# Second attention rewritten as one stream of 32 heads, its key tiles in pairs

## The chip, the cores and the metric

The kernel runs on one core of one Trainium2 chip. The metric is the time on the device in microseconds (us), the median of several runs. One execution was also recorded by the profiler.

## What is computed

The program is two layers of attention and expert feed-forward; the change touches the second attention alone:

```python
query, key, value = (aud_fea, img_fea, img_fea)   # _layernorm(x), ctx_1024, ctx_1024
q = _split_heads(query @ Wq.T, h)
k = _split_heads(key @ Wk.T, h)
v = _split_heads(value @ Wv.T, h)
attn = jnp.einsum('bhnd,bhmd->bhnm', q, k) * scale
attn = jax.nn.softmax(attn, axis=-1)
x = jnp.einsum('bhnm,bhmd->bhnd', attn, v)
```

There are 4 batches of 512 queries and 1,601 keys, 256 channels in 8 heads of 32. The result is added to x.

## The kernel before

`build` (L2156) puts four phases one behind the other, each a block with a barrier at its end: `attention0`, `experts`, `attention1`, `experts`. Here it is `attention1` (L1593) that matters.

**Precision.** Every float32 operand is split into two float16 parts, high and low. A product of projections takes three matmuls (high by high, high by low, low by high, `triple`, L1858). A head has only 32 channels, so the three products of a score are stacked along the contraction: `kst` holds per head 32 rows of high keys, 32 of low, 32 of high again, and a row of ones; `qst` holds high, high and low queries and a row with minus the maximum. One matmul with 97 rows (L1995) then gives the scores of 128 keys by 512 queries, less the maximum. The stacking is done by DMAs from SBUF to SBUF on the SP queue (L1727, L1735).

**Opening** (once). Weights are transposed and split, x of all 4 batches is normalised (L2040 to L2048), transposed, projected to queries and split (L1864 to L1889). Then the transposed and split context, the keys (L1893 on, events below NV0) and the values of batch 0 are made.

**A batch** (`batch`, L1931 on PE). First the values (13 tiles of keys), then the maxima of head 0 alone (L1962), then 8 heads. The maxima of head n+1 are spread over head n: 12 matmuls of 512 keys and 4 of 65 keys into `psA` (two buffers), reduced by DVE (L2108, L2103), combined to one column (`mc`, L2093), turned to a row by 4 transposes (L1946) and written by DVE into `qst` (L2097). Context and keys of the next batch are made during head 7 (`NEXT`); values and first maxima come after its end.

**A head** (`main`, L1987). For each of 13 tiles of keys (12 of 128, the last of 65): the score matmul into `psS` (4 buffers); ACT takes the exp twice, to float32 `pf` (L1831) and to float16 `ph` (L1833); POOL (10 tiles, L1774) or DVE (3 tiles, L2130) subtracts them to `pl`; PE multiplies `ph` and `pl` with the values into `psO` (L1971, L1973), five tiles behind the scores. Each tile of values holds high and low parts and a column of sums in 65 columns. After the last tile ACT copies `psO` to `of` (L1820); PE may overwrite `psO` only after this (`pe.wait_ge(s_oF, ...)` in `pv`). Four float32 matmuls with `fold` (L1983) add high and low and turn the result; DVE divides and adds to x (L2113, L2117). Heads 1 to 6 are a loop on every engine.

Of the kernel before, what the change touches and what calls it, by code (L numbers as in the profile page):

```python
# [24 lines left out]
P = 128  # L25
# [1567 lines left out]
def attention1(nc, X, identf, io):  # L1593

# [5 lines left out]
    NCK = len(KCH)  # L1606
    NQ = KC * NT // 4 + G * B
    NGC = KC * -(-JT // 4)
    NV0 = NGC + G * NCK
    NW = NV0 + JT  # L1610
    NA = 1 + ST * (NCK - 1)
# [3 lines left out]
    LAG = 5  # L1615
    PR = ring(JT, 7)
    SR = ring(JT, 4)
    R, NS = max(PR) + 1, max(SR) + 1
    VT = [2, 6, 10]
    GT = [j for j in range(JT) if j not in VT]  # L1620

    with ExitStack() as ctx:
        def sb(name, shape, dt=F32):
            return ctx.enter_context(nc.sbuf_tensor("c_" + name, shape, dt))

        def sem(name):
            return ctx.enter_context(nc.semaphore("c_" + name))

        wf = sb("wf", [P, 3, G, D])
        wth, wtl = sb("wth", [P, 3, KC, D], F16), sb("wtl", [P, 3, KC, D], F16)  # L1630
        st, mv = sb("st", [P, NT, 6]), sb("mv", [P, NT, 2])
        ve, mhalf, rstd = sb("ve", [P, NT]), sb("mhalf", [P, NT]), sb("rstd", [P, NT])
        qhs, qls = sb("qhs", [P, G, B * S], F16), sb("qls", [P, G, B * S], F16)
        qst = sb("qst", [P, H, B * S], F16)

        ltn = qst[:, 0:H // 2, :].rearrange("p h n -> p (h n)").bitcast(F32).rearrange("p (t c) -> p t c", c=D)
        lth = qst[:, H // 2:H // 2 + KC, :]
        ltl = qst[:, H // 2 + KC:H, :]
        kst = sb("kst", [P, H, M], F16)
        khs, kls = sb("khs", [P, G, M], F16), sb("kls", [P, G, M], F16)  # L1640
        vst = sb("vst", [P, JT, H, VC], F16)
        cx = sb("cx", [P, JT, D])
        cth, ctl = sb("cth", [P, KC, M], F16), sb("ctl", [P, KC, M], F16)
        mx, mc = sb("mx", [P, ST, NCK]), sb("mc", [P, ST])
        pf = sb("pf", [P, R, S])
        ph, pl = sb("ph", [P, R, S], F16), sb("pl", [P, R, S], F16)
        of = sb("of", [VC, S])
        fold = sb("fold", [VC, DH + 1])
        rl = sb("rl", [P, ST])

        psA = [ctx.enter_context(nc.psum_tensor(f"c_psA{i}", [P, 512], F32)) for i in range(2)]
        psS = [ctx.enter_context(nc.psum_tensor(f"c_psS{i}", [P, 512], F32)) for i in range(NS)]
        psO = ctx.enter_context(nc.psum_tensor("c_psO", [P, 512], F32))
        psM = ctx.enter_context(nc.psum_tensor("c_psM", [P, 512], F32))
        ring4 = psA + psS[0:2]
# [15 lines left out]
        s_wL = sem("wL")
        s_k = [sem(f"k{g}") for g in range(G)]
        s_aP = sem("aP")
        s_aF = sem("aF")
        s_mc = sem("mc")
        s_mT = sem("mT")
        s_mr = sem("mr")
# [7 lines left out]
        s_tP = sem("tP")  # L1685
        s_rl = sem("rl")
        s_tF = sem("tF")

        block = ctx.enter_context(nc.Block(no_gpsimd_drain=True))
        NCONST = 6  # L1690
        names = ("L1_xattn_Wq", "L1_xattn_Wk", "L1_xattn_Wv")

        def wait_low(eng, n, j):

            if j in VT:
                eng.wait_ge(s_pL, done(len(VT), n, VT.index(j)))
# [12 lines left out]
        NONE = [[] for _ in range(JT)]

        @block.sync
        def _(sp):
            for i, name in enumerate(names):
                sp.dma_start(wf[:, i, :, :], io[name].rearrange("(g p) c -> p g c", p=P)).then_inc(s_w, 16)
            def load_context(b):
                src = io["ctx_1024"][bass.ds(b, 1), :, :].rearrange("a m c -> (a m) c")
                sp.dma_start(cx[:, 0:MT - 1, :],
                             src[0:(MT - 1) * P, :].rearrange("(t p) c -> p t c", p=P)).then_inc(s_cx, 16)
                sp.dma_start(cx[0:MR, MT - 1, :], src[(MT - 1) * P:M, :]).then_inc(s_cx, 16)

            load_context(0)

            sp.wait_ge(s_uL, 3 + NQ)
            for h in range(H):
                r0 = (h % HG) * DH
                for piece, src in enumerate((qhs, qhs, qls)):
                    sp.dma_start(qst[piece * DH:(piece + 1) * DH, h, :], src[r0:r0 + DH, h // HG, :]).then_inc(s_q, 16)  # L1727
            def stack_keys(b):
                sp.wait_ge(s_sP, (b * H) * JT + JT)
                for g in range(G):  # L1730

                    sp.wait_ge(s_wL, done(NW, b, NGC + (g + 1) * NCK - 1))
                    for u in range(HG):
                        for piece, src in enumerate((khs, kls, khs)):
                            sp.dma_start(kst[piece * DH:(piece + 1) * DH, g * HG + u, :],  # L1735
                                         src[u * DH:(u + 1) * DH, g, :]).then_inc(s_k[g], 16)

            with sp.Fori(0, B - 1) as b:
                stack_keys(b)

                sp.wait_ge(s_wP, done(NW, b, NGC - 1))
                load_context(b + 1)
# [470 lines left out]
```

## Time and profile before

| | us |
|---|---|
| median of 3 runs | 2967.51 (2966.61 to 2968.86) |
| the profiled execution | 2967.55 |
| its span in the profile | 2965.7 |
| second attention, from the first load to the last write (L1714 to L2117) | 1836.4 to 2534.9 |

PE is TensorE's matmuls, PEld its weight loads, DVE VectorE, ACT ScalarE, POOL GpSimd, SP the queue that issues most DMAs. Starts are us from the span's start. In a timeline a line is: start, duration, engine, line of the kernel, instruction, tile written<-tiles read, count, and in brackets the idle time before it with what ended it. Matmuls overlap: one lasts 0.38 us, but the next may start 0.22 us after it, so costs on PE are read as the distance of starts.

### The profile page before, as it was taken

The page shows a single profiled execution, that of the slowest core. Times are in us where ns is not written, and L with a number is a line of the kernel's source. Part 1 is how long each engine was busy: PE and PEld are TensorE (multiplying, and loading weights), DVE is VectorE, ACT ScalarE, POOL GpSimd, SP SyncE. Part 2 cuts the span into 40 slices and gives each one's busy share as a digit, 9 for nine tenths or more (in the row PEclk, how much of TensorE's full clock was granted, in tenths as well). Part 3 has the DMA queues.
Part 4 walks back from the last instruction along what each step waited for, and adds up shares of the span by engine and source line. Part 5 has one row for each costly group of instructions (what it writes and reads, how often), then busy time and mean ns, then how long its engine had stood idle before and what let it go on. Part 6 is the DMA issues. An engine that isn't in the chain of part 4 may idle for free. (4 is left out here: it accounts for less than half of the span.)

```text
span 2965.7 us, 51867 instructions
## 1 busy us (share of the span) xinstructions
PE 2521.8 (85%) x15253; PEld 1505.1 (51%) x15380; DVE 1938.1 (65%) x3676; ACT 1728.1 (58%) x3155; POOL 1535.5 (52%) x1359
## 2 busy tenths in 40 slices
PE   4999999999999999999945991688888888379992
PEld 2455555555555555555424881344344444258882
DVE  5778677776777776677754644675767677656443
ACT  3556656566555665555523750387786868357661
POOL 2576766676676765665744005075665747320004
PEclk9999999999999999999966995799898999579996
DMA  4000000000000000000025413401002010543113
GB/s 130 1 1 1 23 1 1 1 1 23 1 1 1 1 1 1 1 1 1 1 89 180 146 39 97 99 1 30 26 3 52 0 34 0 203 160 117 45 46 93
DMA packets 83500, 122.54 MB, mean 41 GB/s; under 512 B 11139, under 2 KB 67285, under 8 KB 83349
## 3 DMA queue, kind: packets, MB, share of 16 engines
q1 hardware_dynamic: 72020, 86.23, 9.7%
q0 software_dynamic: 9472, 30.16, 3.0%
q10 hardware_dynamic: 1856, 4.19, 0.4%
q8 instruction: 89, 1.46, 0.2%
q14 instruction: 63, 0.51, 0.1%
HBM read 73.23 MB, written 34.34 MB: 36 GB/s over the span
## 5 line engine op out<-in xcount | busy, mean ns | idle before, releaser
L396 POOL TENSOR_TENSOR a_acc<-a_acc,a_pf 128x512 f32<-128x512 f32 (+1 forms) x480 | 644.8, 1343 | 388.0 <-ACT a_pf L524 367.8
L1774 POOL TENSOR_TENSOR c_pl<-c_pf,c_ph 128x512 f16<-128x512 f32 x320 | 386.8, 1227 | 284.7 <-ACT c_ph L1833 282.3
L524 ACT ACTIVATE a_pf<-a_psS 128x1024 f32<-128x1024 f32 (+1 forms) x288 | 281.2, 976 | 303.6 <-PE a_psS L663 300.1
L813 DVE TENSOR_TENSOR a_pl<-a_pf,a_ph 128x512 f16<-128x512 f32 x448 | 404.6, 912 | 27.5 <-ACT a_ph L530 27.5
L789 DVE TENSOR_REDUCE a_mx<-a_psA 128x1 f32<-128x512 f32 x512 | 344.5, 684 | 49.0 <-PE a_psA L600 42.7
L1270 POOL DMA_INDIRECT f_xn<-f_yrows,f_gidx x64 | 60.7, 949 | 506.5 <-DMA f_yrows<-f_xn 487.6
L1831 ACT ACTIVATE c_pf<-c_psS 128x512 f32<-128x512 f32 (+1 forms) x416 | 255.9, 615 | 114.0 <-PE c_psS L1995 110.6
L2108 DVE TENSOR_REDUCE c_mx<-c_psA 128x1 f32<-128x512 f32 x384 | 251.3, 684 | 53.0 <-PE c_psA L1962 51.2
L530 ACT ACTIVATE a_ph<-a_psS 128x1024 f16<-128x1024 f32 (+1 forms) x288 | 281.0, 976 | 0.0
L1833 ACT ACTIVATE c_ph<-c_psS 128x512 f16<-128x512 f32 (+1 forms) x416 | 257.4, 619 | 0.0
L784 DVE TENSOR_TENSOR a_vl<-a_psA,a_vh 128x256 f16<-128x256 f32 (+1 forms) x272 | 115.0, 423 | 167.4 <-ACT a_vh L469 164.4
L1130 DVE TENSOR_TENSOR f_xn<-f_xn 128x256 f16<-128x256 f32 x320 | 132.3, 422 | 130.9 <-ACT f_xn L1106 126.4
L685 PE MATMUL a_psO<-a_pl,a_vh 128*128 128x512 f16 (+1 forms) x544 | 206.7, 380 | 6.9 <-POOL a_pl L401 6.9
L679 PE MATMUL a_psO<-a_ph,a_vh 128*128 128x512 f16 (+1 forms) x544 | 206.9, 380 | 1.0 <-DVE a_ol L818 1.0
L542 PE MATMUL a_psS<-a_qh,a_kh 128*128 128x512 f16 (+1 forms) x544 | 206.6, 380 | 0.9 <-ACT a_mrow L485 0.8
L680 PE MATMUL a_psO<-a_ph,a_vl 128*128 128x512 f16 (+1 forms) x544 | 206.7, 380 | 0.0
L543 PE MATMUL a_psS<-a_ql,a_kh 128*128 128x512 f16 (+1 forms) x544 | 206.7, 380 | 0.0
L544 PE MATMUL a_psS<-a_qh,a_kl 128*128 128x512 f16 (+1 forms) x544 | 206.5, 380 | 0.0
L600 PE MATMUL a_psA<-a_kh,a_qh 128*128 128x512 f16 x512 | 194.3, 380 | 4.7 <-DVE a_kl L778 1.2
L778 DVE SCALAR_TENSOR_TENSOR a_kl<-a_psA,a_bkv,a_kh 128x512 f16<-128x512 f32 (+1 forms) x160 | 105.3, 658 | 133.7 <-ACT a_kh L463 133.6
L1035 PE MATMUL f_psH<-f_xh,f_w 128*128 128x256 f16 x648 | 178.4, 275 | 15.3 <-ACT f_xn L1106 11.7
L1971 PE MATMUL c_psO<-c_ph,c_vst 128*65 128x512 f16 (+1 forms) x416 | 160.8, 386 | 22.7 <-ACT c_of L1820 22.7
(340 smaller groups left out, 6395.2 us busy)
## 6 DMA issues: line engine op xcount, KB each, us to landing
f_stage<-in_L_ffn_w SPq DMA_DIRECT2D x16, 1024.0 KB
f_stage<-in_L_ffn_W SPq DMA_DIRECT2D x16, 1024.0 KB
f_xn<-f_xrows SPq DMA_DIRECT2D x41, 256.0 KB, 2.8
f_yrows<-f_xn SPq DMA_DIRECT2D x40, 256.0 KB, 2.2
c_kst<-c_khs SPq DMA_DIRECT2D x64, 100.1 KB, 2.2
f_xrows<-f_zero POOLq DMA_DIRECT2D x1, 6400.0 KB, 26.4
a_cx<-in_ctx SPq DMA_DIRECT2D x4, 1536.0 KB
c_cx<-in_ctx SPq DMA_DIRECT2D x4, 1536.0 KB
```

The lines of the kernel that those rows point to most:

```text
L396: g.tensor_tensor(acc[0:k, p, :], acc[0:k, p, :], pf[0:k, q % RF, i, :], ALU.add).then_inc(s_acc, 1)
L524: act.activation(pf[0:r, q % RF, 0:k, :], psS[q % 2][0:r, 0:k, :], ACT.Exp, scale=SCALE).then_inc(s_pF, 1)
L530: act.activation(ph[0:r, q % RP, 0:k, :], psS[q % 2][0:r, 0:k, :], ACT.Exp, scale=SCALE).then_inc(s_pH, 1)
L543: pe.matmul(out, hi, xl_, start=False, stop=False)
L679: pe.matmul(psO[:, :], vh[0:r, g % 2, j, vs], ph[0:r, q % RP, i, :], start=(j == 0), stop=False)
L680: pe.matmul(psO[:, :], vl[0:r, g % 2, j, vs], ph[0:r, q % RP, i, :], start=False, stop=False)
L789: v.tensor_reduce(mx[:, n % 2, it, c:c + 1], ps[:, 0:KCH[c][1]], AX.X, ALU.max).then_inc(s_fr, 1)
L813: v.tensor_tensor(pl[0:r, q % RP, i, :], pf[0:r, q % RF, i, :], ph[0:r, q % RP, i, :], ALU.subtract).then_inc(s_pL, 1)
L1774: g.tensor_tensor(pl[0:r, PR[j], :], pf[0:r, PR[j], :], ph[0:r, PR[j], :], ALU.subtract).then_inc(s_pG, 1)
L1831: act.activation(pf[0:r, PR[j], :], psS[SR[j]][0:r, :], ACT.Exp, scale=SCALE).then_inc(s_pF, 1)
L1833: act.activation(ph[0:r, PR[j], :], psS[SR[j]][0:r, :], ACT.Exp, scale=SCALE).then_inc(s_pH, 1)
L2108: v.tensor_reduce(mx[:, it, c:c + 1], psA[what % 2][:, 0:cn], AX.X, ALU.max).then_inc(s_aF, 1)
```

## The change

`attention1` is written anew, in the form that `attention0` has already: no loops, every engine walks the same list. A head is 7 units, six of two key tiles and one of the last 65 keys. On PE a unit has four places: after each of its two scores and after each of the two values that are multiplied there; items are put in these places.

- Scores of a pair go to one `psS` of two banks (two such buffers, three `psA` buffers for all other items, one `psO`); ACT takes exp over 128x1024 at once. Values are multiplied 4 units behind the scores.
- Of the 12 full tiles POOL subtracts 10 and DVE 2. The unit of 65 keys is neither split nor subtracted: ACT writes one exp `pw` in float32, and one float32 matmul multiplies it with float32 values `vf`.
- The copy of `psO` to `of` goes from ACT to DVE (`out_copy`), division is one DVE multiply of 128x128 into `yt`, and POOL adds `yt` to x (`add_to_x`).
- Context, keys, values and queries of batch b+1 (25 items `T`, `K`, `V`, `N`, `Q`, 24 of which pass ACT and all DVE) are spread over heads 0 to 5 of batch b. Maxima of the next batch's first head are made in head 7, like any other's. `kst`, `qst`, `vst` are double for this. x is normalised batch by batch. The context is loaded in pieces of 512 rows into two buffers.
- SP's order is: 4 context loads of batch b, then `stack(b)` with 48 DMAs, then the loads of batch b+1.
- POOL sets two rows of ones (`kst`), before it was one.

```diff
-    LAG = 5
-    PR = ring(JT, 7)
-    SR = ring(JT, 4)
-    R, NS = max(PR) + 1, max(SR) + 1
-    VT = [2, 6, 10]
-    GT = [j for j in range(JT) if j not in VT]
...
+    UNITS = [(j, j + 1) for j in range(0, JT - 1, 2)] + [(JT - 1,)]
+    U = len(UNITS)
+    NB = 3
+    LAG, LATE, RF, RP = 4, 1, 4, 7
+    ON_DVE = {(4, 1), (5, 1)}
+    TOP = U - 1
...
+    WHOLE = U - 1
+    STACK = 6 * 16
...
+    def keys_and_values(b):
+        out = []
+        for c in range(NK):
+            out += [("T", b, c, k) for k in range(KC) if k < parts(c)]
+            out += [("K", b, c, g) for g in range(G) if g < parts(c)]
+            out += [("V", b, u) for u in range(2 * c, min(2 * c + 2, U))]
+        return out
+    def queries(b):
+        return [("N", b, 0), ("N", b, 1), ("Q", b, 0), ("Q", b, 1)]
+    MAXIMA = [(it, c) for c in range(NK - 1) for it in range(ST)]
+    M_AT = [(0, 0), (0, 2), (0, 3), (1, 0), (1, 2), (2, 0), (2, 2), (2, 3), (3, 0), (3, 2), (4, 0), (4, 2)]
+    PREP_AT = [(h, u, p) for h in range(6) for u, p in ((1, 1), (4, 1), (5, 1), (6, 1))]
+    PREP_AT = [(h, u, p) for h, u, p in PREP_AT if (h, u) >= (0, LAG + 1)]
+    def head_items(n):
+        at = [[[] for _ in range(4)] for _ in range(U)]
+        if n + 1 < NH:
+            for (u, p), (it, c) in zip(M_AT, MAXIMA):
+                at[u][p].append(("M", n + 1, it, c))
+            at[TOP - 1][0].append(("L", n + 1))
+            at[TOP - 1][3].append(("X", n + 1))
+        if n >= 1:
+            at[LAG][2].append(("F", n - 1))
+        b, h = divmod(n, H)
+        if b + 1 < B:
+            todo = keys_and_values(b + 1) + queries(b + 1)
+            for i, what in enumerate(todo):
+                hh, u, p = PREP_AT[i * len(PREP_AT) // len(todo)]
+                if hh == h:
+                    at[u][p].append(what)
+        return at
+    OPEN = [("W", 0), ("W", 1), ("W", 2)] + keys_and_values(0)
+    OPEN[9:9] = queries(0)
+    FIRST = [("M", 0, it, c) for it, c in MAXIMA] + [("L", 0), ("X", 0)]
+    AT = [head_items(n) for n in range(NH)]
+    CLOSE = [("F", NH - 1)]
...
+            def stack(b):
+                if b >= 2:
+                    sp.wait_ge(s_sP, uid((b - 1) * H, 0))
+                sp.wait_ge(s_fr, after_dve(("Q", b, G - 1)))
+                for h in range(H):
+                    g, r0 = h // HG, (h % HG) * DH
+                    sp.wait_ge(s_fr, last_keys(b, g) + 1)
+                    for piece, (k, q) in enumerate(((khs, qhs), (kls, qhs), (khs, qls))):
+                        rs = slice(piece * DH, (piece + 1) * DH)
+                        sp.dma_start(kst[rs, b % 2, h, :], k[r0:r0 + DH, g, :]).then_inc(s_stack[h], 16)
+                        sp.dma_start(qst[rs, b % 2, h, :], q[r0:r0 + DH, g, :]).then_inc(s_stack[h], 16)
+            for b in range(B):
+                for c in range(NK):
+                    load_context(b, c)
+                stack(b)
...
+            def low(q, i):
+                r = rows1(tiles_of(q)[i])
+                g.wait_ge(s_pH, high(q))
+                g.tensor_tensor(pl[0:r, q % RP, i, :], pf[0:r, q % RF, i, :], ph[0:r, q % RP, i, :],
+                                ALU.subtract).then_inc(s_pG, 1)
+            def lows(q):
+                for i in range(len(tiles_of(q))):
+                    if (q % U, i) not in ON_DVE and q % U != WHOLE:
+                        low(q, i)
+            def add_to_x(n):
+                b, h = divmod(n, H)
+                g.wait_ge(s_fr, after_dve(("F", n)))
+                xs = X[:, b * ST:(b + 1) * ST, h * DH:(h + 1) * DH]
+                g.tensor_tensor(xs, xs, yt[:, n % 2, :, :], ALU.add).then_inc(s_x, 1)
...
+                    k, r = len(UNITS[u]), rows1(UNITS[u][-1])
+                    places = AT[n][u]
+                    for what in places[0]:
+                        item(what)
+                    act.wait_ge(s_sP, q + 1)
+                    if q >= RF:
+                        if low_dve(q - RF):
+                            act.wait_ge(s_pL, low_dve(q - RF))
+                        act.wait_ge(s_pG, low_pool(q - RF))
+                    if u == WHOLE:
+                        if n >= 1:
+                            act.wait_ge(s_pv, uid(n - 1, WHOLE) + 1)
+                        act.activation(pw[:, :], psS[q % 2][0:r, 0, :], ACT.Exp, scale=SCALE).then_inc(s_pF, 1)
+                    else:
+                        act.activation(pf[0:r, q % RF, 0:k, :], psS[q % 2][0:r, 0:k, :], ACT.Exp,
+                                       scale=SCALE).then_inc(s_pF, 1)
+                    for what in places[1]:
+                        item(what)
+                    if u != WHOLE:
+                        if q >= RP:
+                            act.wait_ge(s_pv, q - RP + 1)
+                        act.activation(ph[0:r, q % RP, 0:k, :], psS[q % 2][0:r, 0:k, :], ACT.Exp,
+                                       scale=SCALE).then_inc(s_pH, 1)
+                    for what in places[2] + places[3]:
+                        item(what)
...
+            def score(n, u, i):
+                q, j = uid(n, u), UNITS[u][i]
+                b, h = divmod(n, H)
+                r = rows1(j)
+                if i == 0:
+                    if q >= 2 and (q - 2) % U == WHOLE:
+                        pe.wait_ge(s_pF, q - 1)
+                    elif q >= 2:
+                        pe.wait_ge(s_pH, high(q - 2))
                     if u == 0:
...
+                        pe.wait_ge(s_fr, after_dve(("X", n)))
+                ins = pe.matmul(psS[q % 2][0:r, i, :], kst[0:KR, b % 2, h, j * P:j * P + r], qst[0:KR, b % 2, h, :],
+                                start=True, stop=True)
+                if i == len(UNITS[u]) - 1:
+                    ins.then_inc(s_sP, 1)
+            def value(q, i):
+                n, u = divmod(q, U)
+                b, h = divmod(n, H)
+                j = UNITS[u][i]
+                r = rows1(j)
+                if u == WHOLE:
+                    pe.wait_ge(s_pF, q + 1)
+                    if h == 0:
+                        pe.wait_ge(s_fr, after_dve(("V", b, u)))
+                    pe.matmul(psO[0:VC, :], vf[0:r, b % 2, h, :], pw[:, :], start=False,
+                              stop=True).then_inc(s_pv, 1)
+                    return
+                if i == 0:
+                    pe.wait_ge(s_pH, high(q))
+                    if u == 0 and n >= 1:
+                        pe.wait_ge(s_oF, n)
+                if h == 0 and i == 0:
+                    pe.wait_ge(s_fr, after_dve(("V", b, u)))
+                w = vst[0:r, b % 2, j, h, :]
+                pe.matmul(psO[0:VC, :], w, ph[0:r, q % RP, i, :], start=(j == 0), stop=False)
+                if i == 0:
+                    if low_dve(q):
+                        pe.wait_ge(s_pL, low_dve(q))
+                    pe.wait_ge(s_pG, low_pool(q))
+                ins = pe.matmul(psO[0:VC, :], w, pl[0:r, q % RP, i, :], start=False, stop=False)
+                if i == len(UNITS[u]) - 1:
+                    ins.then_inc(s_pv, 1)
...
+            def low(q, i):
+                if q < 0 or i >= len(tiles_of(q)) or (q % U, i) not in ON_DVE:
+                    return
+                r = rows1(tiles_of(q)[i])
+                v.wait_ge(s_pH, high(q))
+                v.tensor_tensor(pl[0:r, q % RP, i, :], pf[0:r, q % RF, i, :], ph[0:r, q % RP, i, :],
+                                ALU.subtract).then_inc(s_pL, 1)
+            def out_copy(n):
+                v.wait_ge(s_pv, uid(n, U - 1) + 1)
+                if n >= 1:
+                    v.wait_ge(s_it, IDX[("F", n - 1)] + 1)
+                v.tensor_copy(of[:, :], psO[0:VC, :]).then_inc(s_oF, 1)
```

## Rows read from the trace of the kernel before

**Rows 1.** The page, part 1: busy time of the engines
```profile
PE 2521.8 (85%) x15253; PEld 1505.1 (51%) x15380; DVE 1938.1 (65%) x3676; ACT 1728.1 (58%) x3155; POOL 1535.5 (52%) x1359
```
**Rows 2.** Windows: stretch, length; busy PE, PEld, DVE, ACT, POOL; granted clock; DMA share, GB/s
```profile
1836.40:1925.97 89.57, 51.64 (x264) 30.07 (x265) 58.35 (x111) 25.18 (x49) 15.49 (x9) 0.73 0.42 109
...
2086.93:2247.90 160.97, 137.50 (x690) 69.31 (x691) 111.98 (x213) 123.03 (x246) 96.74 (x80) 0.95 0.10 25
...
2408.90:2534.90 126.00, 107.59 (x509) 52.56 (x507) 89.27 (x167) 107.33 (x214) 96.53 (x80) 0.97 0.00 0
...
200.00:1400.00 1200.00, 1189.37 (x6679) 648.57 (x6785) 877.59 (x1453) 724.00 (x1090) 813.96 (x675) 1.00 0.01 4
```
**Rows 3.** Timeline of PE in steady heads: start, us, instruction, idle before
```profile
1948.81 0.38 PE L1973 MATMUL c_psO<-c_pl,c_vst 128*65 128x512 f16 x1
1949.02 0.98 PE L1983 MATMUL c_psM<-c_fold,c_of 65*128 65x33 f32 x8
1949.84 0.38 PE L1995 MATMUL c_psS<-c_qst,c_kst 97*128 x1
...
1954.66 0.60 PE L1946 MATMUL c_psM<-identf,c_mc 128*1 128x128 f32 x4 [1.18 <-DVE c_mc L2093]
...
1963.35 0.40 PE L1971 MATMUL c_psO<-c_ph,c_vst 128*65 128x512 f16 x1 [0.83 <-ACT c_of L1820]
```
**Rows 4.** Timelines of PE: keys and values of a batch, and a float32 group of the first attention
```profile
2055.03 0.39 PE L1859 MATMUL c_psA<-c_cth,c_wth 128*128 128x512 f16 x1 [1.50 <-DVE c_kls L2077]
...
2065.75 0.27 PE L1861 MATMUL c_psA<-c_wth,c_ctl 128*128 128x256 f16 x1
2065.86 0.27 PE L1859 MATMUL c_psA<-c_wth,c_cth 128*128 128x256 f16 x1
...
48.87 3.61 PE L623 MATMUL a_psA<-a_pf,a_bkv 128*1 128x256 f32 x16
```
**Rows 5.** Timeline of ACT in the first attention: two exp of 1,024 columns
```profile
811.43 1.02 ACT L524 ACTIVATE a_pf<-a_psS 128x1024 f32<-128x1024 f32 x1 [0.17 <-PE a_psS L663]
812.35 1.02 ACT L530 ACTIVATE a_ph<-a_psS 128x1024 f16<-128x1024 f32 x1
```
**Rows 6.** Timeline of DVE in a steady head
```profile
1968.99 1.27 DVE L2108 TENSOR_REDUCE c_mx<-c_psA 128x1 f32<-128x512 f32 x2
1970.30 0.17 DVE L2093 TENSOR_REDUCE c_mc<-c_mx 128x4 f32<-128x16 f32 x1
1971.39 0.68 DVE L2097 TENSOR_SCALAR c_qst<-c_psM 1x512 f32 x1 [0.92 <-PE c_psM L1946]
...
1973.38 0.43 DVE L2103 TENSOR_REDUCE c_mx<-c_psA 128x4 f32<-128x260 f32 x1 [0.40 <-PE c_psA L1955]
```
**Rows 7.** POOL's subtraction by its line (min, median, max ns), and groups by form
```profile
L1774 POOL TENSOR_TENSOR c_pl<-c_pf,c_ph x320: 1147/1155/1609, 1928.0 to 2530.3; 128x512 f16<-128x512 f32 x160
...
L1774 POOL TENSOR_TENSOR c_pl<-c_pf,c_ph 128x512 f16<-128x512 f32 x288 | 351.2, 1236 | 267.9 <-ACT c_ph L1833 265.4 <-PE c_psO L1973 0.2
L362 POOL TENSOR_TENSOR X<-X,a_yt 128x256 f32<-128x256 f32 x128 | 117.7, 940 | 4.3 <-ACT a_yt L495 4.3
```
**Rows 8.** Timeline of PE before and in the first scores
```profile
1882.76 1.09 PE L1913 MATMUL c_psA<-identf,c_cx 128*128 128x128 f32 x8 [1.41 <-DVE c_qls L2065]
...
1914.77 0.57 PE L1955 MATMUL c_psA<-c_kst,c_qst 96*128 96x65 f16 x4 [1.33 <-DVE c_vst L2082]
...
1925.97 0.59 PE L1995 MATMUL c_psS<-c_qst,c_kst 97*128 x1 [1.09 <-DVE c_qst L2097]
```
**Rows 9.** Timelines of POOL and SP in the opening, and SP's key stacking to landing
```profile
1847.25 10.77 POOL L1757 MEMSET c_kst<- 1x12808 f16 x1
...
1910.90 1.24 SPq L1735 DMA_DIRECT2D c_kst<-c_khs  x2
...
DMA to landing us min/median/max: 2.1/2.2/3.7
```
**Rows 10.** Timeline at the end of the second attention
```profile
2531.96 0.59 ACT L1820 ACTIVATE c_of<-c_psO 65x512 f32<-65x512 f32 x1 [1.90 <-PE c_psO L1973]
```

More of the change, by code:

```diff
@@ new lines, in attention1 @@
+    OPEN = [("W", 0), ("W", 1), ("W", 2)] + keys_and_values(0)
[3 more added lines that the diff above has]
+    CLOSE = [("F", NH - 1)]
+    ALL = OPEN + FIRST + [w for at in AT for unit in at for place in unit for w in place] + CLOSE
+    IDX = {w: i for i, w in enumerate(ALL)}
+    N_ACT = {"W": 1, "T": 1, "K": 1, "V": 1, "N": 1, "Q": 1, "M": 0, "L": 0, "X": 0, "F": 0}
+    AH = list(itertools.accumulate(N_ACT[w[0]] - (w[0] == "V" and w[2] == WHOLE) for w in ALL))
@@ L1622, in attention1, with low_pool @@
+    def low_pool(q):
+        n, u = divmod(q, U)
+        return n * PER_POOL + sum(1 for w in range(u + 1) for i in range(len(UNITS[w])) if (w, i) not in ON_DVE and w != WHOLE)
+    NORMED = {"xs": ST, "xa": 2 * ST, "nx": 3 * ST}
+    NORM_AT = {(2, 0): "xs", (2, 2): "xa", (3, 2): "nx"}
+    RSTD_AT = (2, 5)
     with ExitStack() as ctx:
@@ L1647, in attention1 @@
+        ph, pl = sb("ph", [P, RP, 2, S], F16), sb("pl", [P, RP, 2, S], F16)
         of = sb("of", [VC, S])
         fold = sb("fold", [VC, DH + 1])
[L1649 to L1654, printed above, removed]
@@ L1655, in attention1 @@
-        ring4 = psA + psS[0:2]
+        rl = sb("rl", [P, 2, ST])
+        yt = sb("yt", [P, 2, ST, DH])
+        wf = pf[:, 0:2, :, :].rearrange("p a b s -> p (a b s)")[:, 0:3 * G * D].rearrange("p (i g c) -> p i g c", i=3, g=G)
+        psA = [pb(f"psA{i}", [P, 512]) for i in range(NB)]
+        psS = [pb(f"psS{i}", [P, 2, S]) for i in range(2)]
+        psO = pb("psO", [P, S])
         s_const = sem("const")
         s_w = sem("w")
-        s_cx = sem("cx")
+        s_cx = [sem("cx0"), sem("cx1")]
@@ L1675, in attention1 @@
         s_mc = sem("mc")
-        s_mT = sem("mT")
-        s_mr = sem("mr")
         s_sP = sem("sP")
@@ L1723, in _ @@
[L1723 to L1736, printed above, removed]
@@ new lines, in _ @@
+            pe.wait_ge(s_w, 48)
+            for what in OPEN:
+                item(what)
+            pe.wait_ge(s_const, NCONST)
+            pe.wait_ge(s_pool, 3)
+            for what in FIRST:
+                item(what)
+            for n in range(NH):
+                for u in range(U):
+                    q = uid(n, u)
+                    places = AT[n][u]
+                    values = tiles_of(q - LAG) if q >= LAG else ()
+                    for i in range(2):
+                        if i < len(UNITS[u]):
+                            score(n, u, i)
+                        for what in places[i]:
+                            item(what)
+                    for i in range(2):
+                        if i < len(values):
+                            value(q - LAG, i)
+                        for what in places[2 + i]:
+                            item(what)
@@ L2156, in build @@
+            for q in range(NH * U - LATE, NH * U):
+                for i in range(len(tiles_of(q))):
+                    low(q, i)
+            out_copy(NH - 1)
+            for what in CLOSE:
+                item(what)
 def build(nc, io, out, phases):
```

726 lines of the change are left out of this document (310 added, 416 removed).

## The prediction

> **What bounds the kernel now.** I read the page first: PE is busy 85% of the span, no other engine over 65% [rows 1]. The share hides that the phases differ, so the second view is the windows. In a steady stretch of the first attention PE is busy 1,189 of 1,200 us at the full clock of 2.4 GHz; there nothing but PE's work counts [rows 2]. The second attention takes 1836.4 to 2534.9 = 698.5 us and is another thing: an opening of 89.6 us with PE busy 51.6 at a clock of 0.73, three batches of about 161 us, and the last, which has no next batch to prepare, of 126 us, or 15.75 us a head [rows 2]. So a batch costs 35 us more than its eight heads, while POOL works no longer in it than in the last (96.7 and 96.5 us): this is preparation with the exp pipeline empty.
>
> The third view is the timeline of PE in a head, the fourth the same for the other engines. A float16 matmul of 512 columns takes 0.217 us from start to start, the group with `fold` 0.82 [rows 3]. A head has 13 scores, 12 maxima, 26 values (51 x 0.217 = 11.1), the short maxima and the turn of the maximum (about 0.45 each) and `fold`: 12.8 us. The other 3 us are waits: 1.18 for the combined maximum and 0.83 for the copy of `psO` [rows 3], each some 0.2 more from start to start, and steps of the loops. I take all of the change's worth from this phase; the others are not touched.
>
> **The steady head after.** On PE: 13 scores, 12 maxima and 24 values are 49 x 0.217 = 10.63; short maxima 0.45, turn 0.43, `fold` 0.82. The last unit's float32 matmul is in no row. Nearest is the float32 group of the first attention: 8 calls of 256 columns show as 16 records in 3.61 us; less the last one's latency of 0.38 that is 0.215 a record and 0.43 a call [rows 4], so a call of 512 columns is two records of 0.43, 0.86. The bounds are 0.43 (no more than the two float16 matmuls that it replaces) and 0.86 plus 0.2 for its weights. Together 13.2 us, 0.4 more than now: without a split this unit costs PE 0.43 more and spares ACT one exp, POOL one subtraction.
>
> What could stop PE in it, by walking through the seven units:
> - ACT: exp of 1,024 columns follow at 0.92 us [rows 5]; 12 of them and one half are 11.5 us, and `ph` of a unit is done about 2.2 us after its scores, 0.9 before PE wants that `psS` two units later. No wait.
> - POOL: 10 subtractions of 1.24 on the mean [rows 7] and the addition, about 0.5 (half of the 0.94 for 256 columns [rows 7]): 12.9 us. It lags a unit or two; values come four units behind. No wait, but little room.
> - DVE: 12 maxima at about 0.6, short ones 0.43, combining 0.17, the row 0.68 [rows 6], 2 subtractions, the copy of `psO` and the division, about 0.6 each: 10.9 us. It keeps up.
> - The maximum: `L` stands ahead of the second score and four value matmuls. `L` to `X` takes 0.6 to DVE's start, 0.43, 0.17 and hand-overs [rows 6], 1.45 us; PE has 0.45 + 5 x 0.217 = 1.54 to do. The 1.18 goes. From the combined maximum to the end of the row's write are 1.6 us (1970.47 to 1972.07 [rows 6]); PE has 1.5 of work until it needs the row: at most 0.15 left.
> - The copy of `psO` is late next. The float32 matmul stands at place 2 of unit 3; DVE first reduces the maximum behind it, then copies (0.65): about 2.7 us from the matmul's start. PE reaches the first value of the new head 1.74 us after it. It waits **0.9 us**, as much as now. In heads 1 to 5 of a batch an item of preparation of about 1.3 us stands exactly there (unit 4, place 1) and covers it. So 14 heads without items and the 3 heads 0 that have theirs later pay: 17 x 0.9 = 15.3 us. Small rests in the others, 18 x 0.15 = 2.7.
>
> **Preparation** now lies in the stream, but is PE work all the same: keys 36 matmuls at 0.217 and 12 short ones, 8.2 us; values 78 at 0.109 [rows 4], 8.5; 34 transposes at 0.116 ((1.09 - 0.28) / 7 [rows 8]), 3.9; queries 12 x 0.217, 2.6. 23 us a batch, three times: 69. Its 24 evictions on ACT and 25 on DVE (some 12 and 15 us) fit: heads with items last about 17 us on PE, ACT has 13.7 there, DVE 14.
>
> **The opening.** PE's first transposes come at 1841.6 as before, but DVE normalises a quarter of the rows. POOL's memset of one partition's ones takes 10.77 us [rows 9] and is now done twice, to about 1866; nothing but the first maxima waits for it. Weights, queries (5.5 us) and then batch 0 as before: its transposes to its last value took 1882.8 to 1914.8 less a wait of 1.3 = 30.7, I take 32 [rows 8]. That ends at about 1884, its last keys at 1882.5. Now queries too are stacked behind this, 6 DMAs for head 0 at 0.62 and 2.2 to land [rows 9]: 6.1 us. Then maxima alone, 11.2 us as before [rows 8]. First score at 1899.8 instead of 1926.0. Bounds: 23 us of pure PE work after 1845 give 1889; a clock at 1.2 GHz for most of it gives 1912. I take the nearer row, the old batch 0.
>
> **Once more only.** The first head starts at 1.2 GHz, as it did (matmuls with a latency of 0.59 instead of 0.38 [rows 8, 3]), +4.5. SP issues all 48 DMAs of stack(0), 30 us [rows 9], before it loads the context of batch 1: landing about 1916.5, while PE wants it in unit 5 of head 0, about 1910.5. PE waits 6 us and gets some half clock back with it, 8 in all. For later batches the stack starts with head 6 and the load lands before its use. The end (copy, `fold`, division, and now POOL's addition) takes 4.5; before 2.9 from the copy on [rows 10].
>
> **Sum.** 32 x 13.2 = 422.4; 69 preparation; 15.3 and 2.7 waits; 4.5, 8 and 4.5: 526.4 us from the first score. With 63.4 of opening 589.8, against 698.5: **108.7 us less**. The profiled execution took 2967.55 (span 2965.7 and 1.85 around it), which is the median within 0.04. 2967.5 - 108.7 = 2858.8, **2859 us**.
>
> **The rivals.**
> - *Hand-overs do not overlap.* Four engines with 11 to 13 us of work in 14 leave little room, where in the first attention the others had 60 to 73% [rows 2]. At about 1.15 us more for each of 32 heads: +37, 2896. For it: the waits of today. Against: depth four units, and the first attention. Chance 0.17.
> - *POOL becomes the bound.* If its subtractions took the longest seen, 1.609 [rows 7], a head would take it 16.6 us, 2.45 more than the 14.1 of PE with its wait; in the 14 heads without items: +34, 2893. Against: the median is 1.155. Chance 0.08. The Trainium skill, "GPSIMD Engine Reference", section Key points, says that POOL shares its SBUF interfaces with VectorE and names instructions with two SBUF inputs; of these DVE has two a head instead of three, which speaks against it.
> - *The float32 matmul is no dearer than two float16 ones*: 32 x 0.43 = 14 less, or the opening ends 10 us earlier: about 2845. Chance 0.11. This is also the case where the wait for the copy shrinks.
> - *The opening gains nothing* (half clock and stacking behind everything): +26, 2885. Chance 0.06.
> - *Matmuls closer than 0.217.* Were a stream without loops to issue them at 0.131, the 49 would take 6.4 us, PE 9.0, and POOL with 12.9 would set every head: 32 x 12.9 = 413, 17 once only and the opening of 63.4 make 493, or 2762. No row shows a step under 0.215 for 512 columns, and preparation, outside the loop of heads, has the same pace, 0.11 for 256 columns [rows 4]; chance 0. The Trainium skill, "TensorE: Matmul & The Clock Gate", section Back-to-back issue gap, has this 131 ns as the spacing of a sustained stream; the trace does not agree, with 0.217.
> - *Slower.* PE walks its list in order with three `psA`. An item goes PE, ACT, DVE: 0.38 + 0.5 + 0.63 and three hand-overs of 0.2, 2.1 us. If PE stood still that long for each of 75 items, that is 158 us: 3017. It decides from 108.7 / 75 = 1.45 us an item. For it: today's preparation has such waits, 1.50 before a group of keys [rows 4]. Against: no item follows directly on the one it needs, and the first attention passes as many items with 11 us idle in 1,200 [rows 2]. Chance 0.03.
>
> **Numbers.** The forecast has 0.55. The range reaches from the cheap float32 matmul with an early opening, 2836, to hand-overs that do not overlap, 2896; left out are part of that rival, and the slower one. A measurement of this kernel can tell about 0.2%, 6 us: faster 0.96, same 0.01, slower 0.03.
>
> **What would show it.** Right: the distance of two heads' first scores about 14.1 us in heads 6 and 7 and in batch 3, 17 in heads 1 to 5; one wait of about 0.9 for the copy of `psO` a head there and none for the combined maximum; two float32 records of 0.43 apart a head; first score near 1900; one wait for the context of 6 us; no gap between batches. Wrong: `pl` or `ph` named in PE's waits, a granted clock under 1 inside the stream, waits for `psA` items, or POOL without idle time.

## The result and the profile after

The changed kernel takes 2888.97 us (median of 4 runs, 2888.49 to 2889.64), the kernel before beside it 2967.27: a ratio of 0.9736, 95% interval 0.9719 to 0.9752. It is 78.3 us faster, where 108.7 were forecast; 2889 lies in the range and on the forecast side, 30 us above the forecast of 2859.

The page of the changed kernel, part 1, answers to [rows 1]:

```profile
PE 2487.0 (86%) x15253; PEld 1504.2 (52%) x15380; DVE 1947.3 (67%) x3548; ACT 1661.8 (58%) x2669; POOL 1553.2 (54%) x1400
```

The shares hardly moved. The windows answer to [rows 2]: the opening up to the first score, the first head, the rest of batch 0, seven heads of batch 3, and everything after the second attention (columns as in [rows 2]).

```profile
1834.90:1912.94 78.04, 37.88 (x205) 21.74 (x205) 50.13 (x55) 16.09 (x28) 25.20 (x12) 0.70 0.18 50
1912.94:1932.00 19.06, 9.00 (x32) 3.18 (x32) 9.59 (x15) 10.29 (x11) 10.50 (x9) 0.77 0.46 109
1932.00:2054.00 122.00, 114.23 (x613) 63.52 (x614) 96.72 (x166) 90.96 (x109) 77.86 (x72) 0.95 0.11 27
2320.00:2417.00 97.00, 91.36 (x471) 46.92 (x470) 81.63 (x141) 82.75 (x92) 87.66 (x78) 1.00 0.13 30
2458.50:2887.10 428.60, 299.91 (x2599) 255.11 (x2599) 214.67 (x537) 211.84 (x486) 72.52 (x102) 0.84 0.35 115
```

The second attention now lies between 1834.9 and 2458.5 and takes 623.6 us instead of 698.5, 74.9 less. The other 3.7 of the 78.6 that the span lost lie outside the stage: it began 1.5 us earlier, and what follows it took 428.6 instead of 430.8 us. No code is changed there. In this kernel and the nine of the experiments, which share that code, the rest of the program took 2263.6 us (here) to 2266.8. Forecast were 589.8, so 33.8 us are to be explained, and they lie in two places: the opening took 78.0 us instead of 63.4 (14.6 more), the stream behind it 545.6 instead of 526.4 (19.2 more).

The stream itself looks as forecast. PE's waits from 1930 to 2450, in sum, with their number and the longest:

```profile
PE c_psO L2057 <- DVE c_of L2191: 13.9, 21, 0.8
PE c_psA L1960 <- DMA c_cx<-in_ctx: 10.6, 1, 10.6
PE c_psA L1960 <- DVE c_mx L2158: 9.7, 3, 3.2
PE c_psO L2057 <- ACT c_ph L1930: 2.3, 3, 0.8
```

The wait for the combined maximum of [rows 3] is gone; what is left in a steady head is the one for the copy of `psO`. Two lines were not forecast at this size: one wait of 10.6 us for the context, and three of 3.2 before transposes, at DVE's door.

From the starts of the 65-key score of each head (L2033, 97x65), the distance from the head before to this one is, in batch 1: head 0 14.7 us, then 18.9, 18.4, **24.1** (head 3), 18.2, 16.3, 15.2, 13.9. Batches 0 and 2 repeat this within 0.8; in batch 3 each is 13.83 to 13.88. Head 3 stands out in all three batches (23.5, 24.1, 24.3).

**Where the opening went.** The timeline of the changed kernel, all engines, around 1838 (lines selected):

```profile
1838.66 22.50 DVE L2109 TENSOR_SCALAR c_xn<-X,c_mv,c_rstd 128x256 f32<-128x256 f32 x4 [1.85 <-POOL c_rstd L1811]
1838.68 21.62 POOL L1820 MEMSET c_kst<- 1x12808 f16 x2
...
1861.81 1.97 PE L1960 MATMUL c_psA<-identf,c_cx 128*128 128x128 f32 x8 [18.16 <-DVE c_wtl L2125]
```

The normalising of x that DVE starts at 1838.66 ends at 1861.16, less than a microsecond after POOL's two memsets of the ones, which start 0.02 us behind it. PE has transposed its weights and stands still for 18.16 us, because DVE's next piece of work is queued behind the normalising. By its line these four instructions last 427 ns at least and 10,940 at most, each memset 10,766 to 10,802:

```profile
L2109 DVE TENSOR_SCALAR c_xn<-X,c_mv,c_rstd x4: 427/5686/10940, 1838.7 to 1860.7; 128x256 f32<-128x256 f32 x4
...
L1820 POOL MEMSET c_kst<- x2: 10766/10784/10802, 1838.7 to 1849.5; 1x12808 f16 x2
```

**Where head 3 went.** Its timeline, PE, DVE and POOL:

```profile
1982.04 6.93 POOL L1831 TENSOR_TENSOR c_pl<-c_pf,c_ph 128x512 f16<-128x512 f32 x6 [0.18 <-ACT c_ph L1930]
...
1984.08 3.88 DVE L2109 TENSOR_SCALAR c_xn<-X,c_mv,c_rstd 128x256 f32<-128x256 f32 x4
...
1988.62 0.70 PE L1960 MATMUL c_psA<-identf,c_cx 128*128 128x128 f32 x4 [3.25 <-DVE c_mx L2158]
```

The same four instructions, now beside POOL's subtractions of 1.2 us each, take 3.88 us, and PE waits 3.25 us for a buffer that DVE has not yet reduced; the clock falls and stays half until 1995.9, as the next scores show (0.63 us each instead of 0.38).

The theory: **a DVE instruction of this kind (SBUF in, SBUF out) that starts while POOL is at work, or just ahead of it, is held until POOL's running instruction is done.** The rivals: DVE is slow there for a reason of its own (cold data, the wait for `rstd`), or the normalising is only what DVE happens to do while PE waits for something else.

### The profile page after: what moved, and what is told of

Read it like the earlier page. It is cut to its first block and busy times, and to the rows that moved or that the text cites. A ratio compares the mean times of both kernels' runs of the same rounds, so it can differ in the third digit from the quotient of the medians.

```text
span 2887.1 us, 46961 instructions
## 1 busy us (share of the span) xinstructions
PE 2487.0 (86%) x15253; PEld 1504.2 (52%) x15380; DVE 1947.3 (67%) x3548; ACT 1661.8 (58%) x2669; POOL 1553.2 (54%) x1400
## 5 line engine op out<-in xcount | busy, mean ns | idle before, releaser
L1831 POOL TENSOR_TENSOR c_pl<-c_pf,c_ph 128x512 f16<-128x512 f32 x320 | 378.1, 1210 | 173.0 <-ACT c_ph L1930 172.8
L813 DVE TENSOR_TENSOR a_pl<-a_pf,a_ph 128x512 f16<-128x512 f32 x448 | 420.1, 947 | 28.5 <-ACT a_ph L530 28.5
L2158 DVE TENSOR_REDUCE c_mx<-c_psA 128x1 f32<-128x512 f32 x384 | 250.9, 685 | 34.6 <-PE c_psA L2001 32.7
L1923 ACT ACTIVATE c_pf<-c_psS 128x1024 f32<-128x1024 f32 x192 | 197.7, 1030 | 89.8 <-PE c_psS L2033 88.9
L1930 ACT ACTIVATE c_ph<-c_psS 128x1024 f16<-128x1024 f32 x192 | 197.4, 1028 | 0.0
L1035 PE MATMUL f_psH<-f_xh,f_w 128*128 128x256 f16 x648 | 178.6, 276 | 15.4 <-ACT f_xn L1106 11.9
L1037 PE MATMUL f_psH<-f_xh,f_w 128*128 128x256 f16 x648 | 178.4, 275 | 0.0
```

Source lines behind the costliest of these rows:

```text
L813: v.tensor_tensor(pl[0:r, q % RP, i, :], pf[0:r, q % RF, i, :], ph[0:r, q % RP, i, :], ALU.subtract).then_inc(s_pL, 1)
L1035: pe.matmul(ps, a, xh[:, p, k, :], start=(k == 0), stop=False)
L1037: ins = pe.matmul(ps, b_, xh[:, p, k, :], start=False, stop=(k == KC - 1))
L1831: g.tensor_tensor(pl[0:r, q % RP, i, :], pf[0:r, q % RF, i, :], ph[0:r, q % RP, i, :], ALU.subtract).then_inc(s_pG, 1)
L2158: ins = v.tensor_reduce(mx[:, n % 2, it, c:c + 1], ps[:, 0:KCH[c][1]], AX.X, ALU.max)
```

## The experiments

Each is the changed kernel with one edit, run beside the kernel before on the same chip. In 1 to 4 the time is of one run, against 2888.97 (the kernel before beside them: 2967.9); what supports them is the place in the trace, and that they return in 8. By the profiles the second attention alone got shorter by 20.9 us in 1, 17.2 in 2, 19.3 in 3, 10.3 in 4 and 12.6 in 5; the totals say less because the rest of the program took 1.4 to 3.2 us more in these runs.

**1. POOL writes the ones later.** The memsets wait for the whole normalising instead of `rstd`; nothing else moves.

```diff
-                    g.wait_ge(s_rstd, 1)
+                    g.wait_ge(s_st, NORMED["nx"])
```

> POOL sets the two rows of ones only after DVE has finished normalising batch 0. Theory 'held' (DVE's normalising subtraction cannot run while POOL's long memset runs): its 22.50 us fall to about 1.4 (4 x 0.35), PE's wait of 18.2 us before the first transposes of the context shrinks to 1 or 2, and the first score comes some 15 us earlier, 1898 instead of 1912.9; the time falls by 15 (2874). The memset still takes 21.6 us and now ends near 1862, before the first maxima. Rival 'clock and chain' (the opening is long because of half clock and the three-buffer chain): PE just waits elsewhere, less than 5 us are won.

2869.5 us, 19.5 less. The timeline:

```profile
1838.66 1.38 DVE L2109 TENSOR_SCALAR c_xn<-X,c_mv,c_rstd 128x256 f32<-128x256 f32 x4 [1.85 <-POOL c_rstd L1811]
1840.11 21.59 POOL L1820 MEMSET c_kst<- 1x12808 f16 x2 [1.48 <-DVE c_xn L2109]
...
1891.68 0.61 PE L2033 MATMUL c_psS<-c_qst,c_kst 97*128 97x512 f16 x1 [0.78 <-DVE c_qst L2165]
```

The same four instructions, started at the same 1838.66, take 1.38 us instead of 22.50. The memsets last as long as before and PE and DVE do not wait for them. The first score comes at 1891.7, 21.3 us earlier. DVE is not slow by itself; it is what POOL does beside it.

**2. The same memset in sixteen pieces.** POOL and DVE still run side by side. (The count of constants, `NCONST`, goes from 8 to 22 with it.)

```diff
-                                          (vf[:, :, :, 2 * DH:VC], WS), (kst[3 * DH:KR, 0, :, :], 1.0),
-                                          (kst[3 * DH:KR, 1, :, :], 1.0))):
+                                          (vf[:, :, :, 2 * DH:VC], WS),
+                                          *((kst[3 * DH:KR, w, h, :], 1.0) for w in range(2) for h in range(H)))):
```

> The memset of the ones is cut in 16 pieces of one head each (about 1.35 us), and starts where it did, beside DVE's normalising. If DVE is held to the end of the POOL instruction that runs, it gets in between pieces: the 4 subtractions take at most 4 x 1.35 + 1.4 = 6.8 us instead of 22.5, first score 13 to 16 us earlier. If instead POOL's work as such slows DVE in proportion, or DVE waits until POOL's queue is empty, the 4 subtractions still take some 20 us and nothing is won.

2873.7 us, 15.2 less. The timeline, and the normalising by its line:

```profile
1839.78 6.17 DVE L2109 TENSOR_SCALAR c_xn<-X,c_mv,c_rstd 128x256 f32<-128x256 f32 x4 [1.85 <-POOL c_rstd L1811]
1839.80 23.86 POOL L1820 MEMSET c_kst<- 1x1601 f16 x16
...
L2109 DVE TENSOR_SCALAR c_xn<-X,c_mv,c_rstd x4: 1599/1600/1605, 1839.8 to 1844.3; 128x256 f32<-128x256 f32 x4
```

This decides between "POOL slows DVE down" and "DVE is held to the end of an instruction". POOL writes as many ones in as long a time (23.9 us), but each piece is 1.43 us, and now each of the four DVE instructions lasts 1.60, one for one with a piece. The price is the length of POOL's single instruction, not the work beside it.

**3. The next normalising four units later**, at (3, 6) instead of (3, 2).

```diff
-    NORM_AT = {(2, 0): "xs", (2, 2): "xa", (3, 2): "nx"}
+    NORM_AT = {(2, 0): "xs", (2, 2): "xa", (3, 6): "nx"}
```

> DVE's normalising of the next batch is moved from unit 2 of head 3, where POOL has six subtractions back to back, to unit 6, where POOL has 3 us idle. Theory 'held': it takes 1.4 us instead of 3.88, PE's wait of 3.25 us and the half clock behind it (until 1995.9) vanish, and head 3 falls from 23.5 to 24.3 us to about 18.3; three times, so 17 us (2872). Rival (head 3 is long because of the context load or the items' order, not the normalising): head 3 stays at 23 to 24.

2872.8 us, 16.2 less. Where DVE meets no subtraction of POOL's it takes 1.37 us for the four:

```profile
1995.02 1.37 DVE L2109 TENSOR_SCALAR c_xn<-X,c_mv,c_rstd 128x256 f32<-128x256 f32 x4
```

Head 3 takes 16.9 us in all three batches instead of 23.5 to 24.3, and head 4 18.76 instead of 18.16: 6.5 us a batch, and three times that is about the 19.3 of the stage. All other distances stay within 0.8.

**4. The context of batch b + 1 is loaded before batch b is stacked**, its first two chunks.

```diff
-                for c in range(NK):
+                for c in range(2 if b else 0, NK):
                     load_context(b, c)
+                if b + 1 < B:
+                    load_context(b + 1, 0)
+                    load_context(b + 1, 1)
                 stack(b)
```

> SP issues the first two context loads of batch b+1 ahead of the 48 DMAs of stack(b). The wait of 10.6 us for the context in head 0 of batch 0 goes, and the half clock behind it; the first maxima start at most 2 us later because the loads share the DMA engines. 8 to 12 us less (2878). Rival: the loads delay the stacking of head 0 by the time of 1 MB, 4 to 5 us, and half of the gain is lost.

2879.9 us, 9.0 less. PE's waits from 1900 to 2450 no longer have a line for `in_ctx` (lines of code are 3 further here):

```profile
PE c_psO L2060 <- DVE c_of L2194: 13.5, 21, 0.8
PE c_psA L1963 <- DVE c_mx L2161: 9.7, 3, 3.2
PE c_psA L2004 <- DMA c_qst<-c_qls: 5.2, 1, 5.2
```

The third line is not new: the changed kernel has it too, with 5.3 us, ahead of the window shown above. The stage begins at 1834.2 and the first score comes at 1912.2, 78.0 us later as before, so two loads ahead of the stacking cost the opening nothing.

**5. The wait for the copy.** DVE does one maximum (L2158) behind the float32 matmul before it copies `psO`. Here this maximum's place is behind the copy.

```diff
-    M_AT = [(0, 0), ..., (3, 0), (3, 2), (4, 0), (4, 2)]
+    M_AT = [(0, 0), ..., (3, 0), (4, 0), (4, 0), (4, 2)]
```

> Edit: the maximum over tiles that DVE did between the float32 matmul's place and the copy of psO stands one place later, so that DVE copies psO at once. Changed kernel: 2889.0 us; a head without items 13.86 us with one wait of PE of 0.81 us for the copy. Theory A (the copy's place in DVE's order sets this wait): the wait falls to 0.1 to 0.2 us and those 17 heads take about 13.25 us; 17 x 0.6 = 10 us less, 2879. Theory B (another engine's work sets the head at about 13.9 us, POOL's 13 us above all): the wait goes from the copy to another name (ph or pl) and the head stays at 13.8 to 13.9; 2889.

2877.5 us (4 runs, 2876.7 to 2879.7), ratio to the kernel before 0.9694, 0.9679 to 0.9709: 11.5 us less than the changed kernel. In batch 3 a head takes 13.20 to 13.26 us. The window over its seven heads stands beside the same in the changed kernel (97.0 us long, PE busy 91.4):

```profile
2332.60:2425.20 92.60, 92.42 (x471) 46.72 (x470) 85.59 (x141) 82.74 (x92) 87.42 (x78) 1.00 0.04 9
```

PE is busy 92.42 of 92.60 us. The wait came from DVE's order, and no other engine's hand-over stood behind it: theory A.

**6. The last unit split again**, the one part of the change that adds work on PE, undone.

```diff
-    WHOLE = U - 1
+    WHOLE = -1
-        return n * (U - 1) + min(u + 1, U - 1)
+        return q + 1
-    PER_POOL = JT - 1 - PER_DVE
+    PER_POOL = JT - PER_DVE
-                ins = pe.matmul(psO[0:VC, :], w, pl[0:r, q % RP, i, :], start=False, stop=False)
+                ins = pe.matmul(psO[0:VC, :], w, pl[0:r, q % RP, i, :], start=False, stop=(j == JT - 1))
```

(The buffers `vst`, `vf` and `pw` change their sizes with it.)

> Edit: the last unit of 65 keys is again split into two float16 parts: PE has two float16 matmuls (0.43 us) in place of the float32 one (0.86), ACT one exp more a head, POOL one subtraction more and no addition less, 11 x 1.21 + 0.45 = 13.8 us a head instead of 12.5. Theory A (PE's own work sets every head): 0.43 us less in each of 32 heads, 14 us less, 2875. Theory B (POOL is so near that it becomes the bound): heads with items gain 0.43 (18 x 0.43 = 8 us less), heads without items go from 13.86 to 13.8 or more, waits named pl appear; 2881 to 2892. Theory C (the split costs more than it spares, by waits for ACT and POOL in all heads): over 2892.

2901.1 us (4 runs), ratio 0.9774, 0.9759 to 0.9789: **12 us more** than with float32, 8.9 of them in the second attention. Not theory B: waits for `pl` are not among PE's seven largest. Theory C has the size, but not the place, since the loss is not in all heads. Most are faster, by 0.1 to the 0.43 us that PE spares (13.43 instead of 13.86), but head 0 of batches 1 and 2 takes 18.5 instead of 14.7, heads 0, 2 and 5 of batch 3 take 16.0, 17.6 and 14.8 instead of 13.9, and the last head 13.6 instead of 11.0. In head 2 of batch 3 the trace shows why. The timeline of DVE, POOL and PE:

```profile
2372.31 3.61 DVE L2184 TENSOR_TENSOR c_pl<-c_pf,c_ph 128x512 f16<-128x512 f32 x1
2372.69 0.45 POOL L1843 TENSOR_TENSOR X<-X,c_yt 128x128 f32<-128x128 f32 x1
2373.11 3.82 POOL L1831 TENSOR_TENSOR c_pl<-c_pf,c_ph 128x512 f16<-128x512 f32 x3
2375.95 0.68 DVE L2165 TENSOR_SCALAR c_qst<-c_psA 1x512 f16<-1x512 f32 x1
...
2376.78 0.59 PE L2033 MATMUL c_psS<-c_qst,c_kst 97*128 97x512 f16 x1 [2.45 <-DVE c_qst L2165]
```

One subtraction of DVE's lasts 3.61 us (the median in the changed kernel's batch 3 is 0.725). It starts 0.4 us before the end of a subtraction of POOL's and ends 0.55 us after the second of the next three: meanwhile POOL goes through the addition and two subtractions with no idle time between them. Behind it stands the row of maxima, and for that PE waits 2.45 us and loses its clock (0.90 in that head). POOL was not yet what PE waited for, but so dense that DVE found no gap. The other heads lose by the same: PE waits for this row six times between 1930 and 2450, each time behind a held subtraction of DVE's, five times one of 3.55 to 3.61 us and in head 5 of batch 3 one of 2.36. PE's waits, and the window of a steady head:

```profile
PE c_psS L2033 <- DVE c_qst L2165: 13.2, 6, 2.5
...
2404.20:2417.60 13.40, 12.59 (x69) 6.61 (x67) 11.85 (x20) 12.26 (x15) 13.40 (x14) 1.00 0.00 0
```

POOL is busy 13.40 of 13.40 us there.

**7. The same split with one subtraction moved to DVE**, to take the density away. On top of edit 6:

```diff
-    ON_DVE = {(4, 1), (5, 1)}
+    ON_DVE = {(1, 1), (4, 1), (5, 1)}
```

> Edit: the last unit split into two float16 parts as in the run before (2901.1 us), and one subtraction a head (unit 1, second tile) moved from POOL to DVE, so that POOL has 10 subtractions and the addition a head, as in the changed kernel. Theory A (the split lost because POOL had no idle time left, and DVE's subtraction, held beside it, came late: 3.6 us for one): POOL idles again, DVE's subtractions are back at 0.7 to 1.3 us, no wait for qst is left, heads without items take 13.45 us and the others 0.43 less than with float32: 14 us less than 2889.0, 2875. Theory B (the split itself costs, by ACT's exp or by the chain from the last unit to the next head): 2889 or more, with the waits for qst still there. Theory C (DVE has no room for a third subtraction): waits for the copy of psO and for maxima grow, 2885 to 2900.

2902.6 us (4 runs), ratio 0.9788, 0.9773 to 0.9803. Half of theory A holds: the longest wait for `qst` is 0.3 us and no subtraction of DVE's takes over 1.7. But a steady head takes 14.1 us, not 13.45, and three heads (4 and 7 of batch 1, 1 of batch 3) take 1.6 to 1.7 more than their like; why is open. The window of one (13.99 us from score to score) and PE's first wait:

```profile
2348.40:2362.40 14.00, 12.74 (x69) 6.61 (x67) 12.95 (x22) 12.26 (x15) 12.44 (x12) 1.00 0.21 50
...
PE c_psO L2057 <- DVE c_of L2191: 17.8, 21, 1.0
```

DVE is busy 12.95 of 14.0 us, and the copy of `psO` comes 0.2 later still: theory C by its mechanism, though the time is 2.6 us above the range that it gave.

**8. Edits 1, 3, 4 and 5 together.**

> Edit: four small moves together: POOL writes the ones of kst only when DVE has normalised; the next normalising of a batch stands four units later; the context of batch b + 1 is loaded before batch b is stacked; the maximum stands behind the copy of psO. Each alone gave 19.5, 16.2 and 9.0 us less against 2889.0; the fourth about 10 if theory A of it holds. Theory A (each removes a wait of its own, and they add up): 2834, at least 2828 to 2842. Theory B (they remove the same idle time, or an earlier stream runs into the next wait): over 2850.

**2829.8 us** (5 runs, 2827.3 to 2830.1), ratio to the kernel before 0.9532, 0.9519 to 0.9545. That is 59.2 us less than the changed kernel; the four alone gave 19.5 + 16.2 + 9.0 + 11.5 = 56.2. In the second attention alone it is 61.5 against 20.9 + 19.3 + 10.3 + 12.6 = 63.1. They add up: theory A. Windows of the opening and of three heads of batch 3:

```profile
1834.90:1895.01 60.11, 36.88 (x204) 21.46 (x205) 29.88 (x57) 16.09 (x28) 25.16 (x12) 0.76 0.31 85
...
2298.00:2337.70 39.70, 39.60 (x204) 20.00 (x202) 36.70 (x61) 35.45 (x40) 37.50 (x34) 1.00 0.01 1
```

The stage begins at 1836.8 in this run, so that its opening takes 58.3 us. A head is 13.22 us of PE work with PE busy 39.6 of 39.7. This is the best version found.

**9. Edits 6 and 7 on top of that.**

> Edit: the same split and the same third subtraction on DVE, on top of the four small moves (2829.8 us, a head without items 13.22). Theory A (PE's own work is all that is left of a head): 13.22 - 0.43 = 12.8 us a head, 14 less, 2816. Theory B (DVE, with 11.5 us a head and now 0.7 more, or POOL with 12.6, sets the head at about 13.2 or more): 2830 or more, with waits for c_of, c_mx or c_pl.

2837.5 us (5 runs), ratio 0.9563, 0.9550 to 0.9576: 7.7 us more than without them. A steady head takes 13.07 us where PE's work would allow 12.8, and this time POOL has no room left:

```profile
2308.10:2347.30 39.20, 37.87 (x203) 19.89 (x202) 36.70 (x64) 36.92 (x43) 38.85 (x34) 1.00 0.01 1
```

POOL is busy 38.85 of 39.2 us with ten subtractions and an addition a head, 12.95 us. Three of the ten last 1.60 us instead of 1.15: they start while a subtraction of DVE's is in flight, so DVE's third subtraction costs POOL as well (in 8 it was 12.50 us a head with the same ten and the addition). Heads with preparation are slower than in 8 (head 4 takes 19.7 to 21.4 instead of 18.5). Theory B: by its busy time POOL is the bound, while the one wait that PE has in these heads is named for DVE's copy (0.4 us each); that POOL's pace stands behind this wait is argued, not shown.

## Why the prediction was right, and where it was off

**The steady head: right.** 13.2 us of PE work were forecast, 13.22 are measured where PE never waits (8). The step of 0.217 held, so did the float32 unit: forecast were two records of 0.43, and the matmul behind it starts 0.86 us later (2403.26 to 2404.12):

```profile
2403.26 1.02 PE L2047 MATMUL c_psO<-c_pw,c_vf 65*65 65x512 f32 x2
2404.12 0.38 PE L2001 MATMUL c_psA<-c_kst,c_qst 96*128 96x512 f16 x1
...
2405.97 0.38 PE L2057 MATMUL c_psO<-c_ph,c_vst 128*65 128x512 f16 x1 [0.81 <-DVE c_of L2191]
```

The wait for the combined maximum went, and the one for the copy of `psO` stood where it was said, 0.81 instead of 0.9. A head with it takes 13.86 instead of 14.1: the wait costs 0.64 from start to start, since 13.22 is left without it, and in all 11.5 us (5; 12.6 in the stage) where 15.3 + 2.7 = 18.0 were taken.

**Preparation: right in kind, a little small.** The distances of batches 1 and 2 in kernel 8 add up to 130.3 us; less 8 x 13.22 that is 24.6 us a batch instead of 23, 4.7 us in all.

**The context wait: right mechanism, size off.** One wait of 10.6 us, forecast 6; without it 9.0 us are gained (10.3 in the stage), where 8 were taken.

**"Nothing but the first maxima waits for it": the step that failed.** So the prediction put POOL's memset, and costed doing it twice at nothing. What waits for the memset's data is indeed only that. But DVE's normalising, which shares no data with it, is held beside it, and PE behind DVE. This is 19.5 us of the time and 20.9 of the stage (1). The sign stood in the trace of the kernel before. Its memset begins at 1847.25 and takes 10.77 us [rows 9]; the normalising of x beside it, in the timeline and by its line (min, median, max ns), and PE behind it read

```profile
1847.23 16.11 DVE L2048 TENSOR_SCALAR c_qst<-X,c_mv,c_rstd 128x256 f32<-128x256 f32 x16 [3.58 <-POOL c_rstd L1752]
...
L2048 DVE TENSOR_SCALAR c_qst<-X,c_mv,c_rstd x16: 396/400/10940, 1847.2 to 1862.9; 128x256 f32<-128x256 f32 x16
...
1859.51 1.12 PE L1877 MATMUL c_psS<-identf,c_qst 128*128 128x128 f32 x4 [15.05 <-DVE c_qst L2048]
```

By its total it looks like sixteen instructions in 16 us, about one each, while the median is 0.40 us and one lasts 10.94, as long as the memset. The kernel before paid this hold once, 10.9 us with PE waiting behind it; the change, which writes the ones of two sets of keys, pays it twice, and a view that lists the longest beside the median would have said so.

**The next batch's normalising: not costed at all.** "Its 24 evictions on ACT and 25 on DVE (some 12 and 15 us) fit" counted the items and left out the normalising that moves into the stream with them. It cost 16.2 us of the time and 19.3 of the stage (3), by the same mechanism and PE's half clock after it (the granted clock is 0.57 from 1988 to 1996).

**The sum, remade.** It is made of stage times, since the totals hold the rest of the program too. The opening was 14.6 over: 21.3 by the hold (1), less 6.6 because what remains, 1834.9 to 1891.7 = 56.8 us, is shorter than the 63.4 forecast. The stream was 19.2 over: 19.3 for head 3 (3), 4.7 for preparation and 2.3 for the context (10.3 where 8 were taken), less 5.4 for the copy (12.6 where 18.0 were taken) and less 2.2 for the last head, which has no maxima to make and takes 11.0 instead of 13.2. These give 18.7.

**Luck had a part.** The terms that were too small, 21.3 + 19.3 + 4.7 + 2.3, are 47.6 us; with them alone the time would be 2907, outside the range. That it lies inside is owed to terms that were too dear (6.6, 5.4 and 2.2) and to the 3.7 us outside the stage.

**The rivals.** Hand-overs that do not overlap: refuted, PE is busy 92.42 of 92.60 us once the copy is early (5). At 2896 it lay near the measured time all the same, for reasons of another kind. POOL as the bound (2893, as near by chance): not in the changed kernel, where it works 87.7 of 97 us, but it is near, and in 9 it is full. An opening that gains nothing (2885): it gained 11.5 us, 89.6 to 78.0, of 26 forecast, and what it fell short by is the hold, not half clock or stacking. Matmuls closer than 0.217: none in the stream. A cheaper float32 matmul: no, 0.86. And undoing it costs 12 us (6), so the 0.43 us that it adds on PE are well spent; the prediction saw what it spares POOL and gave that no value. Slower, by waits for `psA` at each item: absent but for head 3. The Trainium skill, "GPSIMD Engine Reference", section Key points, was used against the POOL rival: shared SBUF interfaces and contention with DVE instructions that have two SBUF inputs. The page names a second kind beside it, DVE instructions in a 2-port mode. The normalising has one tensor input and one output, both in SBUF and of an even number of columns (256), and by "VectorE: DVE Perf Modes", section What auto-detection actually checks, that is the case for a 2-port mode. The traces agree with the rule (22.50 against 1.38 us), and its price in them is the rest of POOL's running instruction: 10.94 us for one DVE instruction beside a memset of 10.77, 1.60 beside a piece of 1.46.

## What to carry to other kernels

When a step moves, list what each engine does beside it, not only what waits for its data: a POOL instruction of 10 us holds an unrelated DVE instruction that reads and writes SBUF for 10 us. Cut long POOL instructions into short ones, or start them when DVE is at work that reads PSUM (in 1 its instructions from PSUM kept 0.68 to 0.70 us beside the memsets of 10.77), and look in the trace at the longest of a group, not its mean. And an engine near full load costs before the waits name it: with one subtraction more a head, POOL without idle time in 13.4 us, a wait of 2.45 us appeared for another engine's row.

## What the hardware showed that was not expected

- Four DVE TENSOR_SCALAR of 256 float32 columns in SBUF: 1.37 to 1.38 us with POOL idle, 3.88 beside subtractions of 1.2 us, 6.17 beside memsets of 1.43 us, 22.50 beside memsets of 10.8 us. The DVE reductions from PSUM kept their 0.68 to 0.69 us beside a busy POOL.
- A DVE subtraction with two SBUF inputs can stay held over more than one POOL instruction where these follow without a gap: 3.61 us in experiment 6.
- The hold works both ways. Of POOL's 320 subtractions in the changed kernel 36 last 1.60 to 1.67 us and all others at most 1.23 (median 1.16), and the 36 are just those that start while a subtraction of DVE's is in flight and has over 0.2 us to go.
- A POOL memset of 12,808 float16 in one partition takes 10.78 us, 1,601 of them 1.43: about 0.83 ns an element and 0.1 us each.
